# Attention on one core: picked products directly in front of the next weighted ones, small products at new places

## The reference, cut to what matters

```
q = (src @ Wq + bq) in 8 heads of 16;  k = (src @ Wk + bk) in 8 heads of 16
attn = softmax(q k^T / sqrt(16))
out = sum over r in 0..3 of (attn * (adj == r)) @ (src @ Wv[r] + bv[r])
x = layernorm(src + out @ Wo + bo)
ff = gelu(x @ W1 + b1) @ W2 + b2
result = layernorm(x + ff)
```

## Time and profile before

| | |
|---|---|
| median of 3 runs | 1249.26 us (1248.03 to 1250.36) |
| profiled execution, its own time | 1250.93 us, span 1249.1 us |
| busy share of the span | PE 87%, DVE 77%, ACT 59%, POOL 49% |
| peak products, first to last | 458 to 1069 us |
| one steady turn | 39.13 us |

### The profile page before, as it was taken

One profiled execution on the slowest core, in us unless ns is written; L12 is line 12 of the kernel. 1 busy time (PEld: TensorE's weight loads), 2 busy tenths in 40 slices (PEclk: granted clock), 3 DMA queues, 4 the chain that ended last, 5 costly groups with the idle time before them and its releaser, 6 DMA issues. The chain is left out here.

```text
span 1249.1 us, 21656 instructions
## 1 busy us (share of the span) xinstructions
PE 1092.9 (87%) x6087; PEld 501.8 (40%) x6087; DVE 962.1 (77%) x2313; ACT 742.4 (59%) x1341; POOL 614.3 (49%) x515
## 2 busy tenths in 40 slices
PE   4588888888888549999999999999999999979996
PEld 3465665665664312233332333323333233234443
DVE  2878878878877537788888888888888888618777
ACT  3477677677675323666666666666666666644442
POOL 3311311311300135878887788878888787900000
PEclk9799999999998857999999999999999999979998
DMA  5222112112100242321333213332133320000000
GB/s 168 92 76 77 50 63 88 50 54 97 50 1 1 86 118 70 106 66 50 111 110 97 69 53 109 110 93 70 57 109 110 89 73 8 2 0 34 34 34 34
DMA packets 49413, 86.50 MB, mean 69 GB/s; under 512 B 8787, under 2 KB 35795, under 8 KB 44246
## 3 DMA queue, kind: packets, MB, share of 16 engines
q1 hardware_dynamic: 46454, 85.56, 22.3%
q10 hardware_dynamic: 2912, 0.40, 0.2%
HBM read 52.12 MB, written 29.36 MB: 65 GB/s over the span
## 5 line engine op out<-in xcount | busy, mean ns | idle before, releaser
L1387 POOL TENSOR_TENSOR b_picked<-b_prob,b_mask 128x512 f32<-128x512 f32 x384 | 473.4, 1260 | 129.8 <-ACT b_prob L1116 129.7
L1251 DVE TENSOR_REDUCE b_top<-b_peak 128x1 f32<-128x512 f32 x512 | 343.6, 687 | 87.7 <-PE b_peak L1003 82.6
L1116 ACT ACTIVATE b_prob<-b_score 128x1024 f32<-128x1024 f32 x256 | 262.0, 1023 | 193.3 <-PE b_score L1018 191.5
L812 POOL TENSOR_TENSOR a_hw_n<-a_hw,a_inv 128x512 f32<-128x512 f32 x16 | 19.5, 1219 | 274.2 <-DVE a_inv L700 261.1
L1042 PE MATMUL b_o_ps<-b_picked,b_dval 128*32 128x512 f32 x1024 | 136.4, 604 | 12.7 <-DVE b_picked L1265 10.2
L1042 PE MATMUL b_o_ps<-b_prob,b_val 128*32 128x512 f32 x1024 | 136.3, 604 | 0.3 <-ACT b_o_t L1127 0.3
L1265 DVE TENSOR_TENSOR b_picked<-b_prob,b_mask 128x512 f32<-128x512 f32 x128 | 113.0, 883 | 1.5 <-ACT b_prob L1116 1.4
L1003 PE MATMUL b_peak<-shared 96*128 96x512 bf16 x256 | 103.4, 409 | 3.6 <-DVE b_top L1251 3.5
L645 ACT ACTIVATE a_att<-a_att,a_least 128x512 f32<-128x512 f32 x128 | 91.1, 716 | 17.3 <-DVE a_least L673 16.8
L1003 PE MATMUL b_peak<-b_k_stack,b_q_stack 96*128 96x512 bf16 x256 | 98.3, 384 | 0.0
L673 DVE CUSTOM_DVE_ANT_0 a_att<-a_att,a_no_edge 128x512 f32<-128x512 f32 x128 | 97.2, 778 | 0.0
(11 more groups left out here) (176 smaller groups left out, 1807.6 us busy)
## 6 DMA issues: line engine op xcount, KB each, us to landing
a_adj_in<-in_adj SPq DMA_DIRECT2D x16, 1024.0 KB, 5.4
scratch<-shared SPq DMA_DIRECT2D x32, 384.0 KB, 2.6
shared<-scratch SPq DMA_DIRECT2D x16, 768.0 KB, 6.8
scratch<-shared SPq DMA_DIRECT2D x32, 256.0 KB, 2.6
b_q_stack<-scratch SPq DMA_DIRECT2D x8, 768.0 KB, 5.5
b_k_stack<-scratch SPq DMA_DIRECT2D x8, 768.0 KB, 8.0
a_x_in<-in_x SPq DMA_DIRECT2D x16, 256.0 KB, 2.7
xs<-in_x SPq DMA_DIRECT2D x16, 256.0 KB, 5.5
```

Source lines behind the costliest of these rows:

```text
L1116: act.activation(prob[s % 2][:, 2 * u:2 * u + 2, :], score[u][:, :, :], ACT.Exp, scale=float(DH) ** -0.5).then_inc(sem("exp_ready"), 1)
L1251: dve.tensor_reduce(top[g][:, hh, c:c + 1], peak[hh % 2][:, :], AX.X, ALU.max, negate=True).then_inc(sem("peak_read"), 1)
L1387: pool.tensor_tensor(picked[(NR * s + rel) % 2][:, hh, :], prob[s % 2][:, hh, :], m, ALU.mult).then_inc(sem("picked_pool"), 1)
```

## The change

On TensorE the picked group now lags by two steps instead of one (`moved(..., -2)`). In steps 1 and 5 it stands at the head of the step (it closes the sum in `o_ps`, which ScalarE must copy before the next weighted group starts a new one); in the six others it stands directly in front of the weighted group of step s-1, so that eight column-tiled products follow each other. What stood between peak 3 and the next step's peak 0 is gone from there. The table gives the items new places and "late" is gone. Before: q mid of step 0, k mid of 1, top1 early of 2, v0 late of 2, o1 mid of 3, turn_o early and out mid of 4, y mid of 5, top0 early and v1 late of 6, o0 mid of 7. Now: q mid of 0, o1 mid of 1, top1 mid of 2, k early and turn_o mid of 3, v0 early and out mid of 4, y mid of 5, v1 early and top0 mid of 6, o0 mid of 7. ScalarE's first exponential waits for picks and for a new count, `weighed`, instead of `picked_used`; `keep_o` moves to the head of steps 1 and 5. ScalarE does turn_o and y in front of its second exponential, and the masks of the next batch in steps 1 and 2. VectorE does its half of the mid items between its reads of peak 2 and peak 3, but for q in step 0. GpSimd's third part of k moves to step 4.

```diff
--- before.py
+++ after.py
@@ -888,12 +888,12 @@
 
 
         ITEMS = {
-            0: [(0, "mid", "q", 2), (1, "mid", "k", 2), (2, "early", "top1", 0), (2, "late", "v0", 1), (3, "mid", "o1", -1),
...
+            0: [(0, "mid", "q", 2), (1, "mid", "o1", -1), (2, "mid", "top1", 0), (3, "early", "k", 2),
...
         }

         def live(b):
@@ -1021,7 +1021,7 @@
 
                 def weigh(t, par, s, rel):
 
-                    b, par, s = moved(t, par, s, -1)
+                    b, par, s = moved(t, par, s, -1 if rel is None else -2)
                     if not live(b):
                         return
                     g, c = s // C, s % C
@@ -1041,8 +1041,7 @@
                     for hh in range(GH):
                         mm = pe.matmul(o_ps[32 * hh:32 * hh + 32, :], v[:, c, GH * g + hh, :], src[:, hh, :],
                                        start=(c == 0 and rel is None), stop=(c == C - 1 and rel == NR - 1))
-                    if rel is not None:
-                        mm.then_inc(sem("picked_used"), 1)
+                    mm.then_inc(sem("weighed" if rel is None else "picked_used"), 1)
 
                 def item(t, name, by):
                     b = t + by
@@ -1084,21 +1083,27 @@
 
                 def turn(b, par):
                     for s in range(S):
+                        ends = s % C == 1
+                        if ends:
+                            weigh_picked(b, par, s)
                         peaks(b, par, s, 0)
                         scores(b, par, s, 0)
                         for name, by in items(path, s, "early"):
                             item(b, name, by)
                         peaks(b, par, s, 1)
+                        if not ends:
+                            weigh_picked(b, par, s)
                         weigh(b, par, s, None)
                         peaks(b, par, s, 2)
                         scores(b, par, s, 1)
                         for name, by in items(path, s, "mid"):
                             item(b, name, by)
                         peaks(b, par, s, 3)
-                        for rel in range(NR):
-                            weigh(b, par, s, rel)
-                        for name, by in items(path, s, "late"):
-                            item(b, name, by)
+
+                def weigh_picked(b, par, s):
+
+                    for rel in range(NR):
+                        weigh(b, par, s, rel)
                 turns(pe, turn)
             both_paths(pe, run)
 
@@ -1111,14 +1116,16 @@
                     if not live(b):
                         return
                     if u == 0:
-                        past(act, sem("picked_used"), NR * (S * b + s - 1))
+                        past(act, sem("picked_pool"), POOL_HEADS * NR * (S * b + s - 1))
+                        past(act, sem("picked_dve"), (GH - POOL_HEADS) * NR * (S * b + s - 1))
+                        past(act, sem("weighed"), S * b + s - 1)
                     act.wait_ge(sem(f"score_ready{u}"), S * b + s + 1)
                     act.activation(prob[s % 2][:, 2 * u:2 * u + 2, :], score[u][:, :, :], ACT.Exp,
                                    scale=float(DH) ** -0.5).then_inc(sem("exp_ready"), 1)
 
                 def keep_o(b, par, s):
 
-                    b, par, s = moved(b, par, s, -1)
+                    b, par, s = moved(b, par, s, -2)
                     if not live(b) or s % C != C - 1:
                         return
                     g = s // C
@@ -1201,27 +1208,24 @@
 
                 def turn(b, par):
                     for s in range(S):
+                        keep_o(b, par, s)
                         exps(b, s, 0)
-                        if path == 0 and s > 0:
-                            for name, by in items(path, s - 1, "late"):
-                                item(b, par, name, by)
                         for name, by in items(path, s, "early"):
                             item(b, par, name, by)
-                        if s in (1, 2):
-                            second_part(b, s - 1)
-                        if path == 0 and s in (4, 5):
-                            masks(b + 1, (par + 1) % 2, s - 4)
+                        if s in (1, 4):
+                            second_part(b, s // 4)
+                        if path == 0 and s in (1, 2):
+                            masks(b + 1, (par + 1) % 2, s - 1)
                         if s == 6:
                             rstds(b - 1)
+                        if s in (3, 5):
+                            for name, by in items(path, s, "mid"):
+                                item(b, par, name, by)
                         exps(b, s, 1)
-                        for name, by in items(path, s, "early"):
-                            load_tops(b, par, name, by)
-                        for name, by in items(path, s, "mid"):
-                            item(b, par, name, by)
-                        keep_o(b, par, s)
-                        if path == 1:
-                            for name, by in items(path, s, "late"):
+                        if s not in (3, 5):
+                            for name, by in items(path, s, "mid"):
                                 item(b, par, name, by)
+                                load_tops(b, par, name, by)
                         if s == 0:
                             centre(b - 2, (2, 3))
                         if s == 7:
@@ -1346,9 +1350,13 @@
                         for name, by in items(path, s, "early"):
                             item(b, name, by)
                         peaks(b, par, s, 2)
+                        if s > 0:
+                            for name, by in items(path, s, "mid"):
+                                item(b, name, by)
                         peaks(b, par, s, 3)
-                        for name, by in items(path, s, "mid"):
-                            item(b, name, by)
+                        if s == 0:
+                            for name, by in items(path, s, "mid"):
+                                item(b, name, by)
                         if path == 1:
                             pick(b, par, s)
                             if s == 0:
@@ -1396,8 +1404,8 @@
                 def turn(b, par):
                     for s in range(S):
                         pick(b, par, s)
-                        if s in (1, 2):
-                            third_part(b + 2, s - 1)
+                        if s in (1, 4):
+                            third_part(b + 2, s // 4)
                 turns(pool, turn)
             both_paths(pool, run)
         return sem("centred")
```

More of the change, by code:

```diff
@@ L890, in attention @@
         ITEMS = {
-            0: [(0, "mid", "q", 2), (1, "mid", "k", 2), (2, "early", "top1", 0), (2, "late", "v0", 1), (3, "mid", "o1", -1),
[L892 to L896, removed]
+            0: [(0, "mid", "q", 2), (1, "mid", "o1", -1), (2, "mid", "top1", 0), (3, "early", "k", 2),
+                (3, "mid", "turn_o", -1), (4, "early", "v0", 1), (4, "mid", "out", -1), (5, "mid", "y", -1),
+                (6, "early", "v1", 1), (6, "mid", "top0", 1), (7, "mid", "o0", 0)],
+            1: [(0, "mid", "q", 2), (1, "early", "v0", 0), (1, "early", "v1", 0), (1, "early", "v2", 0), (1, "early", "v3", 0),
+                (1, "mid", "o1", -1), (2, "mid", "top1", 0), (3, "early", "k", 2), (3, "mid", "turn_o", -1),
+                (4, "mid", "out", -1), (5, "mid", "y", -1), (6, "mid", "top0", 1), (7, "mid", "o0", 0)],
         }
```

## The result

Median of four runs 1261.3 us (1260.13 to 1262.58), before 1249.02 us (four runs, 1248.03 to 1250.36): ratio 1.0098, 95% interval 1.008 to 1.0115. I had said 1254, 1235 to 1260. The direction held, the size didn't: I had 4.7 over the 1249.3 known then, and it is 12.3. The profiled execution took 1261.1 us, 10.2 more than the one of before, at a mean granted clock of 0.964 against 0.959, so the two can be compared stretch by stretch.

What follows compares the result with a forecast made beforehand. TensorE's own order was taken as the bound. A steady turn of -1.4-0.8+2.4+0.45=+0.65 us, 14 times +9, with start -2 and last turn -1.4, gave +5.6: 1254.9 at the median, taken as 1254 us, range 1235 to 1260.

Steps and rivals of the forecast that it cites:

- Merging saves 0.23 in six steps: TensorE, picked group directly before weighted group: 2.39 us a step against 2.62, saving 1.4 us a turn.
- Rival C: TensorE's merged pair: the second group's weight load shows, 0.7 us a turn, 1264 us; chance 0.04.
- Waits of the picked group gone: TensorE: 0.8 us a turn of waiting, nearly all before step 6's picked group, goes as it comes a step later.
- Stalls: TensorE peaks waiting for VectorE's reads: 0.70 twice (steps 1, 7), 0.64 step 6, 0.18 step 2, small 0.15; 2.4 us a turn.
- The unknown term, DVE's pick in step 6: VectorE's pick held because GpSimd's starts 0.05 us ahead: bounds 0 and 0.5 us a turn, taken as 0.45.
- Rival A: Step 6: VectorE's pick starts before GpSimd's, no collision; 1248.6 us, no change; chance 0.24.
- rival D: More VectorE picks collide, step 7 being only 0.1 us clear: +0.3 us a turn beyond forecast, 1259 us; chance 0.09.
- turns 0 to 14: Steady turns, each +0.65 us, counted 14 times: +9 us.
- Start, -2: Before the first peaks: product k moves to step 3, peaks start 3.7 us earlier, about 1.5 given back.
- rival B: Faster: stalls behind VectorE's reads smaller, 1.2 us a turn, 1232 us; sooner clock rise could add up to 5; chance 0.26.
- Last turn, -1.4: Final turn with almost no peaks: merging's saving kept without stalls, 6 times 0.23 us.
- The sum: Whole run: turns +9, start -2, last turn -1.4, together +5.6 us.

Runs made afterwards that it cites:

- experiment 7: Kernel of 6 with the picked group back at the head of every step, merging alone undone: 1257.85 us, ratio 1.007.
- 6: Changed kernel with the second peak product behind the merged pair, first scores before the first peak, VectorE's order following, b_shift behind step 7's pick: 1237.39 us, ratio 0.9911.
- Experiment 3: Changed kernel with b_shift moved behind VectorE's pick in step 7, instead of before that step's first read: 1253.59 us, ratio 1.0034.
- experiment 5: Changed kernel with the picked group back at the head of every step, all else kept: 1250.03 us, ratio 1.001.
- experiment 2: Changed kernel with VectorE's halves of the mid items moved behind its fourth read: 1251.45 us, ratio 1.0012.
- 8: Kernel of 6 with VectorE's second read in front of its pick again, TensorE's order kept: 1367.48 us, ratio 1.095.

## Why the prediction came out as it did

- **Merging saves 0.23 in six steps: right.** The trace has 0.31, 0.88 and 0.97, as summed (0.98 said for the last), and experiment 7 against 6 gives 1.4 a turn. Rival C is out with it. By the rule on row groups in the Trainium skill (TensorE: Matmul & The Clock Gate, What overlaps and what doesn't) the second group would show its weight load, and in six steps of every turn the trace shows none: 0.88 start to start, not 1.00.
- **Waits of the picked group gone: right** (12.7 to 2.8 us in all).
- **Stalls.** Behind step 1: 1.14 from first score to second peak instead of 0.44, 0.70 as said. Step 6: 0.19+0.47=0.66, said 0.64. Step 2: 0.19, said 0.18. The small ones, at turn_o and in front of the value item of step 4: 0.15 and 0.20, said 0.15 for both together. Step 7: 1.42, said 0.70.
- **The unknown term, DVE's pick in step 6: the first of two steps that failed.** I gave 0.45 to a collision there. It didn't happen; the pick of step 6 was free (0.68). The picks of steps 2 and 7 were held (1.6 and 1.4 to 1.5), the first at next to no cost here. Rival A's condition came true (in step 6 DVE's pick starts at 705.22, GpSimd's at 705.28), and the time went the other way, since the collision was one step on. `b_shift`, an operation on 4 numbers a partition, doesn't occur in my sum. In the kernel before its lowest was 0.16 us, its median 0.52 and its highest 1.12, which could have told me that it is held too. Its hold put the two reads and the pick of step 7 late; "step 7 is only 0.1 clear" (rival D) was the warning, priced at 0.3 a turn more and 9 in 100. Experiment 3 measures the hold with what follows: 0.66 a turn. Without it the turn is 39.32 to 39.45, and my sum without the 0.45 was 39.33. So the mechanism of the stalls was right, and what was wrong is which operation is held, and the price: 0.66 instead of 0.45.
- The Trainium skill (SBUF — State Buffer, SBUF: two separate sides) has VectorE, where it reads two inputs from SBUF, and GpSimd exclude each other, whoever starts first keeping the ports that they share. By that rule the trace agrees: `b_shift` starts with GpSimd's third pick at 707.99 and ends within 0.02 us of it, though it needs 0.14.
- **By place:** turns 0 to 14 +13.0, said +9, the difference being 0.27 a turn (+0.92 for +0.65) over the 14 or 15 turns. My items add up to about 0.2 a turn more than the turn lengths show; that rest I can't assign.
- **Start, -2: near enough, in part by luck.** -3.8, of which 1.5 is stage a, which gave q earlier (451.1 instead of 452.6) without having been changed; that leaves -2.3. The first peak stands at 453.0, the 454.5 that I had said less that 1.5. But two things are in it that the sum did not have: the granted clock was 0.81 from 457 to 468 us and 0.71 from 468 to 476, in the kernel before 0.50 in both (rival B names that), and the first score sat idle for 1.58 us until the transfer of the maxima had landed, of which I had said that it lands before the scores. They pull against each other, and no run takes them apart.
- **Last turn, -1.4: the second step that failed, +1.5.** I took TensorE for its bound. It is GpSimd. GpSimd's row at the end, in the changed kernel:

```profile
1079.19 26.87 POOL L1395 TENSOR_TENSOR b_picked<-b_prob,b_mask 128x512 f32<-128x512 f32 x21 [1.10 <-ACT b_prob L1123]
```

and in the kernel before:

```profile
1068.88 18.63 POOL L1387 TENSOR_TENSOR b_picked<-b_prob,b_mask 128x512 f32<-128x512 f32 x15 [0.88 <-ACT b_prob L1116]
1087.68 7.96 POOL L1387 TENSOR_TENSOR b_picked<-b_prob,b_mask 128x512 f32<-128x512 f32 x6 [0.17 <-ACT b_prob L1116]
```

TensorE in the changed kernel, with the group that waits for its end:

```profile
1103.13 1.04 PE L1042 MATMUL b_o_ps<-b_prob,b_val 128*32 128x512 f32 x8
1106.11 1.07 PE L1042 MATMUL b_o_ps<-b_picked,b_dval 128*32 128x512 f32 x8 [1.94 <-POOL b_picked L1395]
```

  In both kernels GpSimd makes its last 21 picks all but without a break, 1.28 us each and 3.8 a step, while a step of TensorE without peaks would be some 3.3 us long by its distances; a shorter step for TensorE brings nothing. The turn's last picked group stands 34.3 us behind the first score, before 33.1: 1.2 of the 1.5. GpSimd's first pick of the turn starts 2.5 behind the first score instead of 1.9, and the profile has it wait 1.30 for a picked group (`b_o_ps`). That is a price of the picked group's place in the middle of a step, which my sum put at nothing: in the whole run GpSimd waits 43.4 us for picked groups, and at most 0.1 in the kernel before and in experiment 5, where the group stands at the head of every step. The other 0.3 lies behind the last picked group, with the clock (last section).
- **The sum.** Said 5.6; the turns add 4, the last turn 2.9, the start takes 1.8 off and the rest behind stage b 0.6: the measured 10.2, but for 0.1. So of the 4.6 that I was off, the last turn has more than half.
- **Rivals.** B's condition, smaller stalls, did not come true in this kernel; what it priced at 1232 (the fourth read straight behind its peak) is experiment 2, and it gave 1251: 0.54 a turn came back at the small products' one bank and 0.38 at the pick of step 2, and `b_shift` was still held. Rival D is the nearest (1259).

## What to carry to other kernels

A group that is moved was also a spacer: list every pair of operations that it stood between (here peak and read, small product and bank) and the shortest distance each pair can stand, before its saving is counted. The remedy was to keep the saving and place the merged pair where the tightest pair needs it (1237 us), and the order of the reading engine has to follow in the same edit (8: 1367 us). For an operation that may be held by another engine's work, take its highest duration in the trace, not its usual one, however small it is.

## What the hardware showed unexpected

- An operation of 128 by 4 on VectorE takes 0.14 us free and 1.16 beside a pick of GpSimd: its size sets its own 0.14, and where it is held it ends when the other does. In the kernel before it takes 0.52, from 706.71 to 707.23, beside a pick of GpSimd that ends at 707.21.
- The granted clock in the last 9 us of stage b. The stretch in the kernel before:

```profile
1096.00:1105.00 9.00, 5.82 (x22) 2.35 (x14) 1.43 (x3) 1.97 (x5) 0.00 (x0) 0.61 0.00 0
```

and in the unmerged kernel of 5:

```profile
1096.00:1105.00 9.00, 4.07 (x22) 1.65 (x22) 2.46 (x9) 1.76 (x3) 0.00 (x0) 1.00 0.00 1
```

  TensorE waits for 35% of the one and 55% of the other, and yet the first was granted a mean of 0.61, 2.4 GHz up to about 1098 us and 1.2 GHz from there on, and the second 2.4 GHz throughout; from the last picked group to the last product it is 9.3 us in the kernel before, 9.6 in the changed one and 7.3 in this one. Some 2 us of a comparison of single profiles hang on this, and none of the runs shows what decides it.
